# Edge lists in two parts, the mask by four 64x64 products, and the mask one step sooner

## The chip, the cores and the metric

The kernel runs on one NeuronCore of a Trainium2 chip. The metric is the device time of one execution in microseconds (us). Engines are named as in the profile: PE is TensorE's matmul, PEld its weight load, DVE is VectorE, ACT is ScalarE, POOL is GpSimd, SP is SyncE; a "q" behind a name is that engine's sequencer, which issues DMAs.

## The reference

One layer of a graph network over N = 1250 nodes of 512 values, 8 heads of 64, and 41250 edges (`src`, `dst`, sorted by `dst`) with 8 weights each. In short:

```
xn = layernorm(x)
x_norm = layernorm(xn) * g + b;  q, k, v = x_norm @ Wq/Wk/Wv + bias
ws[e, h] = (q[origin] . k[destination])[h] * SCALE * w[e, h]
att = softmax of ws over all edges of one origin
values[origin] += att * v[destination];  gnn = xn + (values @ W1 + b1) @ W2 + b2
mix = linear attention of xn (elu + 1 features), @ Wp + bp
x = x + gnn + mix
out = x + ffn(layernorm(x))      # a small table step on 51 columns
```

## The kernel before

The kernel turns the sparse attention into a dense one. A table `w_tab` in HBM has a row for each of 1280 origins and 1360 columns: 1250 destinations and 110 spare ones ("losers", edges that share a cell with another). Every cell has 8 weights. It is first filled with a marker `EMPTY`, then the weights of the edges are scattered into it.

**The table (SP, DVE, POOL).** SP loads both edge lists into `sW` and `dW` with a halo of 65 (`load_edges`, L410): 22 chunks of 1875 edges on 125 partitions. Chunk 0 needs ten one-row transfers beside. SP then goes through the chunks: it loads the weights of chunk k (`load_weights_of_edges`, L431) and fills a strip of the table with the marker (`empty`, L419). DVE turns the lists into numbers (`edges`, L1187, all 22 chunks in one go) and finds the losers of chunk k (`detect(k)`, L1195: a comparison of 960 values on each partition, a reduction, two small steps), which gives the cells and counts up `s_idx`. POOL scatters 15 rows of cells a chunk (L514), when the chunk's strip, weights and cells are there. After all chunks it gathers the losers' weights (16 transfers, L520), scatters them (16, L525), and then gathers key and value rows of the losers (`KVx`, L587, one of ten for each block of origins, the first three at once).

**The dense start (ACT, PE, DVE).** ACT issues the loads of `x`, then `Wq`, then six short columns (`crow`, L607). PE turns the columns (L903), DVE copies them (L1287), PE folds a bias through `Wq` (`fold(0)`, L873), transposes the normed `x` (L852), and projects q (L884), k, v (L890) in three pieces of 512, 512 and 256 nodes. DVE takes k and v (`take_k` L1276, `take_v` L1281), with a `detect` between each two. `marker_check` (L1208) looks at the edge weights in `V`'s place, so the v tiles wait for it. ACT copies transposed k rows and stores them with v to HBM. All this is in program order on each engine. The linear attention follows, up to 362 us.

**The attention.** 30 rounds w: three groups of destinations (512, 512, and 226 + 110 spare), each over ten blocks c of 128 origins. A round has four steps p = 0 to 3, one for each pair of heads; u = 4w + p. In a step PE does `scores(u)` (two heads, K = 64, side by side in the two row halves of the array, L1085, in the third group also L1088; then the mask, L1090: an identity times `pen`, added to both score banks), `values(u - 2)` (L1118, two heads side by side in the two column halves) and `transposes(u - 1)` (L1100). DVE does `weighted(u)` (scores times weights with the running maximum, twice, L1540, and the shift, L1544), `odd_probs(u - 1)` (a copy that `values` needs, L1549), and at p = 1 of the second and third group `merge(w - 1)` (L1562 to L1574), at p = 2 of the third `scaled`, at p = 3 of the third `added`. ACT does the exponentials (L765) and the other copy (L772). PE does the closing product `ffn` (L1147) at p = 3 of the third group. From round 11 on there is a merge in every round, from round 21 on an `ffn`.

`mask(w + 1)` (L1529) compares one head's weights of the next tile with the marker and writes `pen`, 128 x 512 of bf16, at the end of DVE's step p = 2. It waits for the tile's load. SP loads the tile of w + 1 (`load_tile`, L451) as soon as `weighted` of round w - 1 is through with the same buffer (two buffers `Wt`); the tile is 2048 KB in the first two groups.

Of the kernel before, what the change touches and what calls it, by code (L numbers as in the profile page):

```python
# [8 lines left out]
ALU = mybir.AluOpType  # L9
# [35 lines left out]
GROUPS = ((0, 512), (512, 512), (1024, COLS - 1024))  # L45
READY = (10, 19, 22)
NW = 3 * NT
NU = NW * 4
# [63 lines left out]
def gps_layer(nc, x, src, dst, w_edge, ln_g, ln_b, Wq, bq, Wk, bk, Wv, bv, W1, b1, W2, b2,  # L112
# [3 lines left out]
    with ctx:  # L116
# [127 lines left out]
        KTx = [ar(13312 + 440 * i, 440).rearrange("p (k n) -> p k n", k=KC) for i in range(2)]  # L244
        pen = [ar(14192 + 256 * i, 256).bitcast(BF16) for i in range(2)]
        tb = ar(14704, 512)
        fo = ar(19520, 512)
# [29 lines left out]
        s_pad = sem("pads_ready")  # L277
        s_edges = sem("edges_loaded")
        s_x = [sem(f"x_loaded{j}") for j in range(3)]
# [58 lines left out]
        s_wl = [sem(f"tile_loaded{i}") for i in range(2)]  # L338
        s_pen = sem("mask_ready")
        s_s = sem("scores_ready")  # L340
        s_ttr = sem("weighted_ready")
# [64 lines left out]
        def _(sp):  # L406
# [3 lines left out]
            def load_edges():  # L410
                for a, to in ((src, sW), (dst, dW)):
                    sp.dma_start(to[:, 1:NCH, :], view(a, CE - HALO, ((CJ, QL), (CE, NCH - 1), (1, WIN)))).then_inc(s_edges, 16)
                    sp.dma_start(to[5:QL, 0, :], view(a, 5 * CJ - HALO, ((CJ, QL - 5), (1, WIN)))).then_inc(s_edges, 16)
                sp.wait_ge(s_pad, 1)
                for a, to in ((src, sW), (dst, dW)):
                    for q in range(5):
                        sp.dma_start(to[q:q + 1, 0, HALO - CJ * q:WIN], view(a, 0, ((1, 1), (1, CJ * (q + 1))))).then_inc(s_edges, 16)

            def empty(k):  # L419
# [11 lines left out]
            def load_weights_of_edges(k):  # L431
                if k > 4:
                    scattered(sp, max(k - RING + 1, (k - 3) * 5 // 8))
                sp.dma_start(pay[:, k % RING, :, :], wq[k]).then_inc(s_pay[k % 4], 16)

            sp.dma_start(sWk, wv(Wk)).then_inc(s_w4[1], 16)
            load_edges()
            for k in range(3):
                load_weights_of_edges(k)
                empty(k)  # L440
            sp.wait_ge(s_idx, 1)
            sp.dma_start(wchk, w_edge.rearrange("(p t) h -> p t h", p=QL)).then_inc(s_chk, 16)
# [31 lines left out]
            with sp.If(sp.value_load(flag[0:1, 0:1], min_val=0, max_val=P) > 0):  # L474
                scattered(sp, NCH - 1)
                sp.wait_ge(s_xs, 16 * SLOTS)

            for w in range(NW):
                load_tile(w)
            for b in range(2):  # L480
# [4 lines left out]
        def _(pool):  # L485
# [20 lines left out]

            for k in range(NCH):
                if k >= 2:
                    pool.wait_ge(s_sc[k % 2], 16 * CJ * (k // 2))
                pool.wait_ge(s_empty[k % 4], emptied(k))  # L510
                pool.wait_ge(s_pay[k % 4], 16 * (k // 4 + 1))
                pool.wait_ge(s_idx, k + 1)
                for j in range(CJ):
                    pool.indirect_dma_start(out=w_tab, out_offset=bass.IndirectOffsetOnAxis(ap=idx[:, k, j:j + 1], axis=0),  # L514
                                            in_=pay[:, k % RING, j, :], in_offset=None,
                                            bounds_check=CELLS - 1, oob_is_err=False).then_inc(s_sc[k % 2], 16)

            pool.wait_ge(s_lists, 2)
            for j in range(SLOTS):
                pool.indirect_dma_start(out=wx[:, j, :], out_offset=None, in_=w_edge,  # L520
                                        in_offset=bass.IndirectOffsetOnAxis(ap=e_idx[:, j:j + 1], axis=0),
                                        bounds_check=E - 1, oob_is_err=False).then_inc(s_wx, 16)
            pool.wait_ge(s_wx, 16 * SLOTS)
            for j in range(SLOTS):
# [67 lines left out]
        def _(act):  # L592
# [11 lines left out]
            act.dma_start(XRES[:, 2:4, :], x[2 * P:4 * P, :].rearrange("(t p) d -> p t d", p=P)).then_inc(s_x[0], 16)  # L604
            act.dma_start(sWq, wv(Wq)).then_inc(s_w4[0], 16)
            for i, a in enumerate((ln_g, ln_b, bq, bk, mbq, b1)):
                act.dma_start(crow[KC * i:KC * i + KC, :], a.rearrange("(k p) -> k p", p=P)).then_inc(s_col, 16)  # L607
            load_x(1)

# [218 lines left out]
        def _(pe):  # L828
# [242 lines left out]
            def scores(u):  # L1071
                w, p = u // 4, u % 4
                g, c = w // NT, w % NT
                d0, n = GROUPS[g]
                if p == 0:
                    pe.wait_ge(s_pen, w + 1)
                    if g == 2:
                        pe.wait_ge(s_kxe, c + 1)
                bs = [bank[SB[(2 * u + hh) % 3]] for hh in range(2)]
                if u >= 1:  # L1080
                    pe.wait_ge(s_ttr, 2 * u - 1)
                qs = [QT[64 * hh:64 * hh + 64, p, c * P:(c + 1) * P] for hh in range(2)]
                m = min(n, N - d0)
                for hh in range(2):
                    mm(bs[hh][:, 0:m], qs[hh], KT[64 * hh:64 * hh + 64, p, d0:d0 + m], start=True, stop=False)  # L1085
                if g == 2:
                    for hh in range(2):
                        mm(bs[hh][:, m:n], qs[hh], KTx[c % 2][64 * hh:64 * hh + 64, p, :], start=False, stop=False)  # L1088
                for hh in range(2):
                    last = mm(bs[hh][:, 0:n], identb[:, :], pen[w % 2][:, 0:n], start=False, stop=True)  # L1090
                last.then_inc(s_s, 1)
# [85 lines left out]
        def _(dve):  # L1177
# [8 lines left out]

            def edges():  # L1187
                dve.wait_ge(s_edges, 16 * 14)
                v.tensor_copy(oc[:, :, :], sW[:, :, HALO:WIN])
                ch.link(v.tensor_copy(dc[:, :, :], dW[:, :, HALO:WIN]))  # L1190
                v.scalar_tensor_tensor(out=key, in0=sW, scalar=float(N), in1=dW, op0=ALU.mult, op1=ALU.add)
                v.tensor_copy(dwin, dW)
                ch.link(v.scalar_tensor_tensor(out=cell, in0=oc[:, :, :], scalar=float(COLS), in1=dc[:, :, :], op0=ALU.mult, op1=ALU.add))

# [92 lines left out]
            v.tensor_copy(cols[:, :, :].rearrange("p i k -> p (i k)"), bank[7][:, 32:32 + 6 * KC]).then_inc(s_cols, 1)  # L1287
            normed(0)
            dve.wait_ge(s_cols, 1)
            take_x(0)  # L1290
            fold(0)
            moments(1)
            normed(1)
            edges()
            detect(0)
            detect(1)
            fold(1)
# [226 lines left out]
            def mask(w):  # L1524
                n = GROUPS[w // NT][1]
                dve.wait_ge(s_wl[w % 2], 16 * (w // 2 + 1))
                if w >= 2:
                    dve.wait_ge(s_s, 4 * (w - 1))
                v.tensor_scalar(pen[w % 2][:, 0:n], Wt[w % 2][:, 0:n, 0], EMPTY, -BIG, ALU.is_equal, ALU.mult).then_inc(s_pen, 1)  # L1529

# [115 lines left out]
            for u in range(NU + 8):  # L1646
# [9 lines left out]
                if p == 2 and 2 * NT < w <= NW:  # L1656
                    scaled(w - 1 - 2 * NT)
                if p == 2 and w < NW - 1:
                    mask(w + 1)
# [42 lines left out]
```

## Time and profile before

| | us |
|---|---|
| median of 3 runs (lowest, highest) | 853.5 (851.43, 857.59) |
| the profiled execution's own time | 854.37 |
| its span in the profile | 851.2 |
| PE, DVE, ACT, POOL busy | 782.4, 583.2, 339.6, 457.5 |
| attention begins (first mask on DVE) | 361.96 |

The profile is of one execution, 3.2 us of whose time lie outside the span. Busy times are sums over the span. The chain view goes back from the last instruction to what released each one. In timeline rows the bracket gives the engine's idle time just before and what ended it.

### The profile page before, as it was taken

The numbers are of one execution on the slowest core, as the hardware profiler recorded it, in microseconds if no ns is written. First come the engines' busy times: TensorE is split into PE (matmuls) and PEld (weight loads), VectorE is DVE, ScalarE is ACT, GpSimd is POOL, SyncE is SP. The second block draws the span as 40 slices with busy tenths as digits, with TensorE's granted clock in tenths as the row PEclk, the third lists the DMA queues.
The fourth block names the chain that finished last, engine by engine and source line by source line (L and its number), as shares of the span: only waits on it lengthen the run. The fifth ranks groups of instructions, "written<-read, shape, count | busy, mean of one in ns | idle before, by whom it ended". The sixth has DMA issues, their size and how long they took to land.

```text
span 851.2 us, 13484 instructions
## 1 busy us (share of the span) xinstructions
PE 782.4 (92%) x4751; PEld 458.3 (54%) x4791; DVE 583.2 (69%) x1331; ACT 339.6 (40%) x794; POOL 457.5 (54%) x391
## 2 busy tenths in 40 slices
PE   2999897899999999979999999999999999999993
PEld 2554445444446444435555555555556667666661
DVE  3487594954233503358888888998988978878886
ACT  0311301022312122035556555556555555545662
POOL 1028878778778877777777787777610001001000
PEclk9989999998999999979999999999999999999998
DMA  7697968897546569315353535435354143242203
GB/s 225 175 375 269 320 203 277 250 357 227 161 136 200 158 185 335 95 15 193 103 202 104 185 120 160 146 103 193 108 164 165 66 152 104 95 148 89 86 1 120
DMA packets 69632, 143.98 MB, mean 169 GB/s; under 512 B 20537, under 2 KB 54251, under 8 KB 65599
## 3 DMA queue, kind: packets, MB, share of 16 engines
q1 hardware_dynamic: 47084, 119.42, 39.9%
q0 software_dynamic: 13344, 6.28, 6.6%
q10 hardware_dynamic: 9136, 17.39, 6.2%
q8 instruction: 40, 0.66, 0.3%
q14 instruction: 28, 0.23, 0.1%
HBM read 77.99 MB, written 64.77 MB: 168 GB/s over the span
## 4 chain that ended last, share of the span: by engine, by line
PE 70%; DVE 21%; DMA 4%; issue 3%; ACTq 1%; ACT 1%; DVEq 0%
PE bank L890 17%; PE bank L884 12%; DVE AR L1540 11%; PE bank L1118 8%; PE bank L1085 8%; PE bank L1100 8%; PE bank L1090 4%; PE bank L1147 4%; DVE AR L1549 3%; DMA AR<-w_tab 2%; PE bank L998 2%; PE bank L873 1%; DMA AR<-in_L_gnn_b_dram 1%; PE bank L987 1%; PE bank L949 1%
## 5 line engine op out<-in xcount | busy, mean ns | idle before, releaser
L514 POOL DMA_INDIRECT w_tab<-pay,idx x330 | 403.9, 1224 | 153.3 <-issue 153.0
L765 ACT ACTIVATE AR<-AR,nmx 128x512 f32<-128x512 f32 (+1 forms) x240 | 159.0, 664 | 48.0 <-DVE nmx L1544 46.5
L1540 DVE CUSTOM_DVE_ANT_0 AR<-bank,AR,MX 128x512 f32<-128x512 f32 (+1 forms) x160 | 151.8, 986 | 20.0 <-PE bank L1090 19.1
L772 ACT ACTIVATE AR<-bank 128x512 f32<-128x512 f32 (+1 forms) x120 | 67.3, 561 | 173.9 <-PE bank L1100 173.9
L1085 PE MATMUL bank<-KT,QT 64*128 64x512 f32 (+1 forms) x480 | 118.3, 570 | 8.6 <-issue 5.3
L1100 PE MATMUL bank<-ident,AR 128*128 128x128 f32 (+2 forms) x880 | 122.7, 280 | 1.1 <-ACT AR L765 1.1
L1118 PE MATMUL bank<-AR,V 128*64 128x128 f32 (+1 forms) x1600 | 114.0, 280 | 6.1 <-DVE AR L1549 6.0
L884 PE MATMUL bank<-AR 128*128 128x512 f32 (+1 forms) x288 | 109.0, 538 | 7.3 <-ACT QT L642 3.2
L1118 PEld LDWEIGHTS bank<-AR,V 128*64 128x64 f32 (+1 forms) x1600 | 85.6, 136 | 52.3 <-issue 50.9
L890 PE MATMUL bank<-AR 128*128 128x512 f32 x240 | 108.3, 607 | 2.5 <-ACT AR L696 2.5
L1100 PEld LDWEIGHTS bank<-ident,AR 128*128 128x128 f32 (+2 forms) x880 | 94.0, 139 | 22.3 <-issue 15.9
L1540 DVE CUSTOM_DVE_ANT_0 AR<-bank,AR 128x512 f32<-128x512 f32 x80 | 83.9, 1086 | 29.7 <-PE bank L1090 29.6
L587 POOL DMA_INDIRECT AR<-kv_rows,xd x10 | 10.8, 1075 | 163.2 <-PE bank L1118 157.7
L884 PEld LDWEIGHTS bank<-AR 128*128 128x128 f32 x288 | 55.5, 195 | 56.2 <-issue 48.4
L890 PEld LDWEIGHTS bank<-AR 128*128 128x128 f32 x240 | 46.0, 195 | 57.3 <-issue 54.6
L1549 DVE COPY AR<-bank 128x512 f32<-128x512 f32 (+1 forms) x120 | 76.7, 639 | 0.2 <-PE bank L1100 0.2
L1090 PE MATMUL bank<-AR,identb 128*128 128x512 bf16 (+1 forms) x200 | 58.4, 358 | 6.5 <-DVE AR L1549 4.3
L1085 PEld LDWEIGHTS bank<-KT,QT 64*128 64x128 f32 x480 | 36.6, 186 | 35.9 <-issue 24.1
L1090 PEld LDWEIGHTS bank<-AR,identb 128*128 128x128 bf16 x240 | 13.7, 97 | 66.4 <-issue 62.1
L765 ACT ACTIVATION_READ_ACCUMULATOR AR<-AR,nmx 128x1 f32 x240 | 45.0, 188 | 0.0
L1147 PE MATMUL bank<-AR 128*128 128x512 f32 x80 | 36.1, 594 | 0.8 <-DVE AR L1581 0.8
L890 PE MATMUL bank<-AR,QMN 128*128 128x512 f32 x80 | 35.9, 593 | 0.5 <-DVE QMN L1444 0.5
(250 smaller groups left out, 755.2 us busy)
## 6 DMA issues: line engine op xcount, KB each, us to landing
w_tab<-ztile SPq DMA_DIRECT2D x20, 2280.0 KB, 15.0
AR<-w_tab SPq DMA_DIRECT2D x20, 2048.0 KB
AR<-w_tab SPq DMA_DIRECT2D x10, 1344.0 KB
w_tab<-ztile SPq DMA_DIRECT2D x3, 1800.0 KB, 13.2
w_tab<-pay,idx POOLq DMA_INDIRECT x330, 4.4
w_tab<-ztile SPq DMA_DIRECT2D x2, 1700.0 KB, 16.5
kv_rows<-AR ACTq DMA_DIRECT2D x9, 256.0 KB, 6.5
kv_rows<-V ACTq DMA_DIRECT2D x9, 256.0 KB
```

The costliest lines, as they stand in the source:

```text
L514: pool.indirect_dma_start(out=w_tab, out_offset=bass.IndirectOffsetOnAxis(ap=idx[:, k, j:j + 1], axis=0), in_=pay[:, k % RING, j, :], in_o ...
L765: act.activation(ws[u % 2][hh][:, 0:n], ws[u % 2][hh][:, 0:n], ACT.Exp, bias=nmx[:, u % 4, hh:hh + 1], accum_out=DG[g][:, c, 2 * p + hh:2 ...
L772: act.activation(PT[u % 2][0][:, 0:nb * P], bank[2][:, 0:nb * P], ACT.Copy).then_inc(s_ea, 1)
L884: last = mm(b[:, 0:n], w[:, k, m * P:(m + 1) * P], src_t(k), start=(k == 0), stop=(k == KC - 1))
L890: last = mm(b[:, :], src_t(k), w[:, k, :], start=(k == 0), stop=(k == KC - 1))
L1085: mm(bs[hh][:, 0:m], qs[hh], KT[64 * hh:64 * hh + 64, p, d0:d0 + m], start=True, stop=False)
L1090: last = mm(bs[hh][:, 0:n], identb[:, :], pen[w % 2][:, 0:n], start=False, stop=True)
L1100: last = nc.tensor.transpose(bank[2 + hh][0:rws, i * P:(i + 1) * P], ws[u % 2][hh][:, a:a + rws], ident[:, :])
L1118: last = mm(bank[4 + w % 2][64 * hh:64 * hh + 64, p * P:(p + 1) * P], v, PT[u % 2][hh][0:rws, i * P:(i + 1) * P], start=(i == 0), stop=(i ...
L1147: last = mm(bank[7][:, :], tb[:, k * P:(k + 1) * P], W12[:, k, :], start=(k == 0), stop=(k == KC - 1))
L1540: v.tensor_tensor_reduce(out=ws[u % 2][hh][:, 0:n], in0=bank[SB[(2 * u + hh) % 3]][:, 0:n], in1=Wt[w % 2][:, 0:n, h], scale=1.0, scalar=MX ...
L1549: v.tensor_copy(PT[u % 2][1][:, 0:nb * P], bank[3][:, 0:nb * P]).then_inc(s_ed, 1)
```

## The change

- The edge lists are loaded and turned in two parts: chunks 0 to 3 first, 4 to 21 after. SP's order becomes: first part, weights and fill of chunk 0, `Wk`, second part, then chunks 1 and 2 as before. DVE does the first part and `detect(0)` before `take_x(0)`, `detect(1)` before `moments(1)`, the second part where all of it stood.
- SP waits for `s_idx` 3 in place of 1 before it loads over the edge lists.
- ACT issues the six columns ahead of `Wq`.
- POOL gathers the losers' weights ahead of chunk 20, in place of after chunk 21.
- The mask product: an identity of 64 x 64 in each quarter of the array, four products of 512 columns in place of two of 128 x 128. Two of them need `pen` with its partition halves swapped: two DMAs of 64 partitions a round, issued by SP (`swap_halves`), into `pens`. PE waits for them at p = 0.
- `mask(w + 1)` moves from DVE's step p = 2 to p = 1, and also waits that the swap of two rounds ago is through. SP's order in the attention becomes swap of w, load of tile w + 1.

```diff
+FIRST = 4
...
+        pens = [bias_row[1 + i][:, 0:256].bitcast(BF16) for i in range(2)]
...
             def load_edges():
                 for a, to in ((src, sW), (dst, dW)):
-                    sp.dma_start(to[:, 1:NCH, :], view(a, CE - HALO, ((CJ, QL), (CE, NCH - 1), (1, WIN)))).then_inc(s_edges, 16)
+                    sp.dma_start(to[:, 1:FIRST, :], view(a, CE - HALO, ((CJ, QL), (CE, FIRST - 1), (1, WIN)))).then_inc(s_edges, 16)
...
+            def load_other_edges():
+                for a, to in ((src, sW), (dst, dW)):
+                    sp.dma_start(to[:, FIRST:NCH, :], view(a, FIRST * CE - HALO, ((CJ, QL), (CE, NCH - FIRST), (1, WIN)))).then_inc(s_edgesb, 16)
...
+            load_edges()
+            load_weights_of_edges(0)
+            empty(0)
             sp.dma_start(sWk, wv(Wk)).then_inc(s_w4[1], 16)
-            load_edges()
-            for k in range(3):
+            load_other_edges()
+            for k in range(1, 3):
                 load_weights_of_edges(k)
                 empty(k)
-            sp.wait_ge(s_idx, 1)
+            sp.wait_ge(s_idx, 3)
...
+            def swap_halves(w):
+                n = GROUPS[w // NT][1]
+                sp.wait_ge(s_pen, w + 1)
+                if w >= 2:
+                    sp.wait_ge(s_s, 4 * (w - 1))
+                for i in range(2):
+                    sp.dma_start(pens[w % 2][64 * i:64 * i + 64, 0:n], pen[w % 2][64 - 64 * i:128 - 64 * i, 0:n]).then_inc(s_pens[w % 2], 16)
+
+            load_tile(0)
+            load_tile(1)
             for w in range(NW):
-                load_tile(w)
+                swap_halves(w)
+                if 1 <= w < NW - 1:
+                    load_tile(w + 1)
...
             for k in range(NCH):
+                if k == NCH - 2:
+                    pool.wait_ge(s_lists, 1)
+                    for j in range(SLOTS):
+                        pool.indirect_dma_start(out=wx[:, j, :], out_offset=None, in_=w_edge,
...
-            act.dma_start(sWq, wv(Wq)).then_inc(s_w4[0], 16)
             for i, a in enumerate((ln_g, ln_b, bq, bk, mbq, b1)):
                 act.dma_start(crow[KC * i:KC * i + KC, :], a.rearrange("(k p) -> k p", p=P)).then_inc(s_col, 16)
+            act.dma_start(sWq, wv(Wq)).then_inc(s_w4[0], 16)
...
+                if p == 0:
+                    pe.wait_ge(s_pens[w % 2], 32 * (w // 2 + 1))
                 for hh in range(2):
-                    last = mm(bs[hh][:, 0:n], identb[:, :], pen[w % 2][:, 0:n], start=False, stop=True)
+                    for to in range(2):
+                        a, b = 64 * hh, 64 * to
+                        last = mm(bs[hh][b:b + 64, 0:n], identb[a:a + 64, a:a + 64], (pen if hh == to else pens)[w % 2][a:a + 64, 0:n], start=False, stop=True)
...
             normed(0)
+            edges(0, FIRST)
+            detect(0)
             dve.wait_ge(s_cols, 1)
             take_x(0)
             fold(0)
+            detect(1)
             moments(1)
             normed(1)
-            edges()
-            detect(0)
-            detect(1)
+            edges(FIRST, NCH)
             fold(1)
...
                 if w >= 2:
                     dve.wait_ge(s_s, 4 * (w - 1))
+                    dve.wait_ge(s_pens[w % 2], 32 * (w // 2))
...
-                if p == 2 and w < NW - 1:
+                if p == 1 and w < NW - 1:
                     mask(w + 1)
```

## Rows read from the trace of the kernel before

**Rows 1.** The chain that ended last, 0 to 60 us: start, us, what.
```profile
5.79 9.94 DMA AR<-in_L_gnn_b_dram
...
16.57 6.96 PE bank L873 x32
...
29.47 14.02 PE bank L884 x32
```
**Rows 2.** Timeline of SP's queue, 0 to 60 us: start, us, what it issues.
```profile
1.79 20.65 SPq L413 DMA_DIRECT2D V<-in_src_dram  x1
```
**Rows 3.** DMA queues, 4 to 16 us: packets, MB, share of 16 engines.
```profile
q10 hardware_dynamic: 1565, 3.00, 77.4%
q1 hardware_dynamic: 873, 0.71, 19.3%
```
**Rows 4.** The same view, 18 to 28 us.
```profile
q1 hardware_dynamic: 2996, 0.95, 40.0%
```
**Rows 5.** The same view, 46 to 52 us.
```profile
q1 hardware_dynamic: 1623, 2.19, 104.4%
```
**Rows 6.** Timeline of DVE, up to 82 us.
```profile
42.13 0.33 DVE L1189 CAST oc<-V 125x330 f32<-125x330 int32 x1 [5.47 <-DMA V<-in_dst_dram]
...
47.35 1.15 DVE L1198 TENSOR_REDUCE QMN<-QMN 125x15 f32<-125x960 bf16 x1
...
56.83 0.75 DVE L1276 TENSOR_SCALAR KT<-bank,kbias 128x512 f32<-128x512 f32 x1 [3.02 <-PE bank L884]
...
81.18 0.46 DVE L1210 TENSOR_SCALAR QMN<-V 125x330 f32<-125x330 f32 x1 [4.25 <-DMA V<-in_edge_attr_dram]
```
**Rows 7.** The chain in the first group, 425 to 442 us: one step of PE.
```profile
432.60 1.06 PE bank L1085 x4
433.66 0.54 PE bank L1090 x2
434.20 1.02 PE bank L1118 x16
435.22 1.02 PE bank L1100 x8
```
**Rows 8.** Timeline of SP's queue in the first group: the issue of one tile.
```profile
425.54 0.32 SPq L463 DMA_DIRECT2D AR<-w_tab  x1
```
**Rows 9.** Windows: length, each engine's busy us (instructions), PE clock, DMA share, GB/s.
```profile
427.50:433.40 5.90, 5.74 (x49) 3.47 (x46) 5.10 (x12) 2.94 (x9) 4.68 (x5) 1.00 0.84 317
433.40:434.00 0.60, 0.60 (x4) 0.11 (x2) 0.21 (x1) 0.60 (x3) 0.30 (x2) 1.00 0.00 0
```
**Rows 10.** Timeline of DVE in the first group.
```profile
432.93 0.68 DVE L1549 COPY AR<-bank 128x512 f32<-128x512 f32 x1
434.34 1.09 DVE L1540 CUSTOM_DVE_ANT_0 AR<-bank,AR 128x512 f32<-128x512 f32 x1 [0.73 <-PE bank L1090]
...
437.16 0.61 DVE L1529 TENSOR_SCALAR AR<-AR 128x512 bf16<-128x512 f32 x1
```
**Rows 11.** The chain in the second group, 556 to 573 us.
```profile
563.70 1.15 DVE AR L1540
...
571.69 1.09 PE bank L1118 x16
```
**Rows 12.** Timeline of DVE in the second group: the mask.
```profile
571.46 0.62 DVE L1529 TENSOR_SCALAR AR<-AR 128x512 bf16<-128x512 f32 x1
```
**Rows 13.** The chain in the third group, 694 to 711 us.
```profile
702.13 0.83 DVE AR L1540
...
708.81 0.88 PE bank L1118 x12
```
**Rows 14.** The chain over the whole span: a tile's load in the second group.
```profile
620.69 13.98 DMA AR<-w_tab
```
**Rows 15.** Timeline of POOL: its first scatter, and the first gather of losers' rows.
```profile
57.47 1.39 POOL L514 DMA_INDIRECT w_tab<-pay,idx  x1 [53.06 <-issue]
...
617.51 1.14 POOL L587 DMA_INDIRECT AR<-kv_rows,xd  x1 [4.92 <-issue]
```
**Rows 16.** POOL's scatters by source line: from issue to landing.
```profile
DMA to landing us min/median/max: 2.4/4.4/9.2
```

More of the change, by code:

```diff
@@ L277, in gps_layer @@
         s_pad = sem("pads_ready")
-        s_edges = sem("edges_loaded")
+        s_edges = sem("first_edges_loaded")
+        s_edgesb = sem("other_edges_loaded")
         s_x = [sem(f"x_loaded{j}") for j in range(3)]
@@ L339, in gps_layer @@
         s_pen = sem("mask_ready")
+        s_pens = [sem(f"mask_halves_swapped{i}") for i in range(2)]
         s_s = sem("scores_ready")
@@ L507, in _ @@
             for k in range(NCH):
+                if k == NCH - 2:
+                    pool.wait_ge(s_lists, 1)
+                    for j in range(SLOTS):
+                        pool.indirect_dma_start(out=wx[:, j, :], out_offset=None, in_=w_edge,
+                                                in_offset=bass.IndirectOffsetOnAxis(ap=e_idx[:, j:j + 1], axis=0),
+                                                bounds_check=E - 1, oob_is_err=False).then_inc(s_wx, 16)
                 if k >= 2:
@@ L516, in _ @@
                                             bounds_check=CELLS - 1, oob_is_err=False).then_inc(s_sc[k % 2], 16)
+            pool.wait_ge(s_wx, 16 * SLOTS)
             pool.wait_ge(s_lists, 2)
[L519 to L523, printed above, removed]
             for j in range(SLOTS):
@@ L1185, in _, with edges @@
             v.memset(wx[:, :, :], 0.0)
[L1187 to L1193, printed above, removed]
+            def edges(a, b):
+                if a == 0:
+                    dve.wait_ge(s_edges, 16 * 14)
+                else:
+                    dve.wait_ge(s_edgesb, 32)
+                v.tensor_copy(oc[:, a:b, :], sW[:, a:b, HALO:WIN])
+                ch.link(v.tensor_copy(dc[:, a:b, :], dW[:, a:b, HALO:WIN]))
+                v.scalar_tensor_tensor(out=key[:, a:b, :], in0=sW[:, a:b, :], scalar=float(N), in1=dW[:, a:b, :], op0=ALU.mult, op1=ALU.add)
+                v.tensor_copy(dwin[:, a:b, :], dW[:, a:b, :])
+                ch.link(v.scalar_tensor_tensor(out=cell[:, a:b, :], in0=oc[:, a:b, :], scalar=float(COLS), in1=dc[:, a:b, :], op0=ALU.mult, op1=ALU.add))
             def detect(k):
```

## The prediction

> **What bounds the kernel now.** I read the chain of waits first, over the whole span and then in short windows. At the start it hangs on the last short column, which lands 9.9 us after its issue; then `fold(0)` at 16.57 and the q projection at 29.47 [rows 1]. From there to the attention PE hardly pauses, so what PE starts sooner stays sooner. In the first group of the attention the chain is PE alone: a step is 1.06 + 0.54 + 1.02 + 1.02 = 3.64 us, a round 14.6 [rows 7], and DVE idles 0.73 in a step [rows 10]. In the second group the chain changes engines: from DVE's `weighted` of p = 1 (563.70) DVE alone leads to PE's `values` at 571.69, 7.99 us [rows 11]; the other 7.5 of a round's 15.5 are PE, two steps. In the third group the DVE part is 702.13 to 708.81, 6.68 [rows 13], of a round of 16.3. These DVE parts hold the merge, which stands at p = 1. POOL bounds nothing: its gather at 617.51 [rows 15] is well ahead of the third group.
>
> **The start.** Columns ahead of `Wq`, and `Wk` (1 MB) no longer ahead of everything. Between 4 and 16 us the DMA engines were full (77.4 + 19.3%) and q10, ACT's queue with x and `Wq`, moved 3.00 MB [rows 3], 250 GB/s. Without `Wk` beside it `x` should land 1.5 to 2 us sooner, the columns before 11, and `Wq` (1 MB, 4 us at that rate) at 12 to 13. `fold(0)` then starts when DVE has copied the columns and `Wq` is there, at about 13.5 in place of 16.57: 3 us gained. Bounds: 5 us gained (it follows the columns alone), 1 lost (the fill of chunk 0, 3.4 MB, halves `Wq`'s rate). I take 3, nearest to [rows 3].
>
> On DVE `edges(0, 4)` (4/22 of the work, about 1 us) and `detect(0)` (two steps of 1.15 and two small ones, 2.7 [rows 6]) come ahead of `take_x(0)`. DVE has them between about 16 and 20, and `take_x(0)` is due at 23: hidden, if the first lists are there by 19. They are 1000 packets; SP's queue managed 873 in 12 us beside ACT's [rows 3] and 300 per us alone [rows 4], so 10 to 16. `detect(1)` (2.7) ahead of `moments(1)` is hidden behind 14 us of q projection [rows 1].
>
> The second part of the lists is what moves later. Before, the issue of the lists held SP for 20 us [rows 2] and DVE had them at 42.13 after 5.47 of waiting [rows 6]. Now 3.4 MB of fill stand in front, 9.3 us at 2.19 MB in 6 us [rows 5]: I expect them at 52 (50 to 57). Behind DVE's wait stand `fold(1)`, the order checks and `take_k(0, 0)`; with 3.4 + 2.2 us of work that comes at 58, where PE, 3 us sooner, has the product ready at 54. PE does not wait for it, since v's first product needs that bank some 13 us later. By the time DVE reaches the v tiles it waited 4.25 us for the weights to check [rows 6], and this room takes up the rest. SP's later count (3 of `s_idx`) comes at about 62, when its queue is still full of fills. Cost 0; each us past 57 costs one.
>
> **POOL.** Its first scatter moves from 57.47 to about 25, but chunk 1 needs the fill behind the second part, at about 62 where chunk 1 began at 80. It ends some 18 to 20 us sooner; nothing waits for that. The gather of loser weights only changes its place. What it does move is the gather of losers' rows: at 617.51 [rows 15] it stretched one tile load to 13.98 us [rows 14] from some 8, for which the mask at p = 2 waited 1.3. It will come near 597, again beside a tile load more likely than not (8 of 15 us are loads), and the mask at p = 1 is due 9 to 10 us after a load's issue in this group. I add 1.5 (between -1.3, no collision, and 4).
>
> **The mask product.** Four products of 512 columns, 64 x 64, in place of two. The trace shows no 64 x 64. Nearest rows: two row halves run side by side (four 512-column passes in 1.06, 0.27 each [rows 7], where the full array takes 14.02/32 = 0.44 [rows 1]), and two column halves as well (16 passes of 128 columns in 1.02, as many us as 8 transposes [rows 7]). One product with its switch is 0.54/2 = 0.27. Bounds: 0.27 (all at once) and 1.08 (one after another). I take 0.36, one product and 0.03 for each that starts behind it, since both halvings are seen to overlap: 0.18 gained a step, in the third group 0.13.
>
> A rule of the Trainium skill speaks against it ("TensorE: Matmul & The Clock Gate", Part 3: Packing small matmuls): a weight load overlaps running matmuls only where the row group differs. By it the two quarters of one row half would take turns and the product would gain nothing. Rows 7 disagree for column halves, which share all rows and still take half the time; by the rule the sum is rival B's.
>
> **The swap.** Two DMAs of 64 KB a round. The mask will be done some 6 us before `scores` of the next p = 0 ask for it; the scatters, small as well, land in 2.4 to 9.2 us, median 4.4 [rows 16]. Cost 0, up to 0.3 a round in a bad case. PE's wait has only PE's own queue behind it.
>
> **The mask one step sooner.** First group (rounds 0 to 10, no merge): the load is issued at 425.54 [rows 8], the DMA engines run until about 433.4 and then stand still [rows 9], so it lands about 8.0 after its issue. DVE would reach the mask after the copy of p = 1 at 432.93 + 0.60 = 433.53 [rows 10], 8.0 after the issue, and, with steps 0.18 shorter, at 7.7. So it waits 0.3, then 0.55, against a slack of 0.73 - 0.18: `weighted` of p = 2 comes about 0.4 late, PE can take 0.2 of it. A round gains 4 x 0.18 - 0.2 = 0.5, eleven rounds 5.7.
>
> Second group (rounds 11 to 20, nine such): the mask now stands behind the merge, inside the DVE part of the chain, in front of `weighted` of p = 2 and the copy that `values` waits for. Before it stood behind that copy (571.46 against PE's 571.69 [rows 11, 12]). The DVE part grows by 0.54, the PE part shrinks by 2 x 0.18: +0.18 a round, +1.6. The load is there (it has 9 us). Third group, nine rounds: the mask of 336 columns adds 0.38, two PE steps give back 0.26: +0.12, +1.1.
>
> **Sum:** -3 - 5.7 + 1.6 + 1.1 + 1.5 = -4.5. The profiled execution becomes 854.4 - 4.5 = 849.9; it was 0.9 above the median of the runs, so 849.0.
>
> **Rivals.**
> A, the forecast, 849.0, 66%; its own range 843 to 855.
> B, the four products overlap only in pairs: the group stays at 0.54. No gain in the first group, +0.54 x 9 and +0.38 x 9 in the others, with -3 and +1.5: +6.8, 860.3, slower. Place: L1090. For it: two quarters share one row half's stream, and no row shows both halvings at once. Against it: rows 7. Some 74 steps count (44 + 18 + 12), so the change loses as soon as the group takes over 0.36 + 4.5/74 = 0.42. One after another (1.08) would be 38 us more than now. 13%.
> C, the second part of the lists comes at 64, since its 320-byte packets starve beside ACT's loads (873 packets in 12 us [rows 3] against 2996 in 10 [rows 4]): `take_k` and `take_v` hold PE, 7 us: 856. Against it: between 18 and 28 us ACT's queue is empty, and 3000 of the 4500 packets fit into such a stretch. 13%.
> D, the mask's new place costs nothing and PE bounds every step: 80 x 0.18 + 40 x 0.13 = 19.6, with -3 and +1.5: 833. Against it: rows 11 and 13, where no PE work stands in the DVE part. 8%.
> That the change does what it says in POOL's order is sure and worth nothing here.
>
> **How the numbers follow.** A measurement of this kernel tells about 1% (8.5 us) from no change: 845 and 862 are the marks. Faster by more: D, and a good fifth of A where the start gives 5 and the group takes 0.30: 0.28. Slower: the worse half of B, a little of C and of A: 0.12. The rest 0.60. The range 840 to 861 leaves out D and the worse half of B.
>
> **What would show it.** The q projection starts at 26 to 27; the first `detect` stands before it; DVE's second part starts at 50 to 57 and PE has no new gap before 130. A step of the first group takes 3.45 to 3.5 us, L1090's share 0.36. DVE has a short wait of the mask on the tile load in rounds 1 to 10 (0.3). Second-group rounds are 15.6 to 15.7, third-group 16.4, with the mask right behind L1574. POOL's first loser-row gather is near 597. Wrong: L1090 above 0.42 a step, a PE gap near 60 to 85 us behind `take_k` or `take_v`, or rounds of the second group under 15.3.

## The result, and the profile after

| | us |
|---|---|
| kernel before, median of its runs beside this comparison | 853.1 |
| changed kernel, median of 4 runs (857.66 to 861.48) | 860.14 |
| ratio, with its 95% interval | 1.0076 [1.0053, 1.0099] |
| forecast | 849.0, range 840 to 861 |
| profiled execution after: own time, span | 857.66, 855.9 (before 854.4, 851.2) |

Here and below, executions over 1.5% slower than the fastest of their kernel are left out (two of r3, one of r14).

The change makes the kernel 7 us slower, where I expected it to be 4 us faster; the profiled execution after is itself 2.5 us below its median. Now from the start of the span to its end, by when `weighted` (L1574, once L1540) begins each part. The first round of the attention begins 3.3 us later than before (371.83 against 368.57), round 10 only 0.3 later (514.81 against 514.52), round 20 later by 4.0 (673.55 against 669.53), and the end by 4.7. So the attention's first group wins 3.0 (forecast 5.7), but the start and the second group lose.

**The start works, and its lead is gone 150 us later.** The chain that ended last, 0 to 55 us (start, us, what; here and below the pieces called issue of under 0.1 us are left out):

```profile
5.30 8.37 DMA AR<-in_L_gnn_Wq_dram
13.72 6.99 PE bank L898 x32
...
42.67 0.50 ACT AR L658
43.21 1.14 PE bank L877 x8
44.35 6.23 PE bank L898 x32
50.58 11.76 PE bank L909 x22
```

`fold(0)` starts at 13.72 in place of 16.57 [rows 1], and now waits for `Wq`. The q projection follows at 26.45, 3.0 sooner than [rows 1] have it. At 43.21 the chain passes through ACT (L658): `detect(1)` stands in front of `moments(1)`, so ACT is late with the tiles that the second x transposes need, and PE waits 1.45 us. That little pause comes with more, as the windows of the stretch show (us, busy time of each engine with its instructions, PE clock, DMA share, GB/s), of the changed kernel:

```profile
43.00:55.00 12.00, 11.79 (x46) 9.14 (x47) 0.00 (x0) 1.73 (x4) 5.74 (x5) 0.57 0.50 118
```

PE is granted 0.57 of its clock here, with 1.2 GHz (a granted 0.5) lasting 10.2 us from 44.7; in the kernel before it lasted 6.8 us from 48.6. `fold(1)` takes 6.39 us where it took 4.67, and k's projection begins at 50.44 against 50.87 (both by the timeline of PE): of 3.0 us, 0.4 are left. Some of it comes back in small waits (2.1 ahead at 161.5). DVE's second part of the lists is where I had it, with no wait of PE behind it. The timeline of DVE:

```profile
56.40 0.30 DVE L1221 CAST oc<-V 125x270 f32<-125x270 int32 x1 [19.56 <-DMA V<-in_dst_dram]
```

The large loss is at 162. The chain, 160 to 190 us, in the changed kernel:

```profile
162.28 14.21 DMA AR<-in_L_mix_Wk_dram
176.49 4.07 issue
180.56 0.56 PE bank L952 x2
```

This is the `Wk` of the linear attention (`L_mix_Wk`, 1 MB; the expectations below also call it the second layer's). It takes 14.2 us to land. Before, the same load took 7.8 (165.1 to 172.9), and no one waited for it. It is not the last that PE waits for: in the kernel PE waits for `Wk` and `Wv` together, ahead of L952, and the 4.07 of issue are the rest of `Wv`'s load. ACT issues `Wv` right behind `Wk`:

```profile
163.17 2.20 ACTq L707 DMA_DIRECT2D AR<-in_L_mix_Wv_dram  x1
```
```profile
AR<-in_L_mix_Wv_dram ACTq DMA_DIRECT2D x1, 1024.0 KB, 17.3
```

163.17 + 17.3 is 180.47, and PE starts at 180.56; before, `Wv` took 10.5 and was there at 176.1, 3 us before PE came to it. Where `Wk` is named below, `Wv` lands 3 to 6 us after it, and where PE waits it is `Wv` that ends the wait. SP's queue shows what is different:

```profile
161.69 0.52 SPq L437 DMA_DIRECT2D w_tab<-ztile  x1
162.31 1.11 SPq L442 DMA_DIRECT2D pay<-in_edge_attr_dram  x1
163.47 2.21 SPq L437 DMA_DIRECT2D w_tab<-ztile  x1
```

Two fills of 2.3 MB stand right beside it. In the kernel before, SP issued a fill at 154.68 and the next at 178.24, so that `Wk` and `Wv` went through between them. The fills wait for POOL's scatters of an earlier chunk, POOL's chunk 1 now starts at 64 in place of 81, and with that the whole sequence of fills lies elsewhere against ACT's loads. The timeline of PE has the price, and the windows the clock behind it:

```profile
180.56 0.56 PE L952 MATMUL bank<-QMN,tri 125*125 125x10 f32 x2 [5.07 <-issue]
```
```profile
177.80:184.60 6.80, 4.04 (x8) 2.36 (x9) 2.63 (x11) 4.66 (x7) 5.41 (x5) 0.50 1.05 390
```

PE idles 5.07 us and then runs 6.8 us at half clock, while the DMA engines are full (share 1.05). A lead of 2.1 has become a lag of 3.3.

**The mask's product.** The chain in the first group, 443 to 447 us, against [rows 7]:

```profile
443.65 1.06 PE bank L1110 x4
444.71 0.34 PE bank L1119 x4
445.05 1.02 PE bank L1147 x16
446.08 1.02 PE bank L1129 x8
```

0.34 us for four products, where two of the full array took 0.54; 0.36 was my term. All four run at once, by the timeline of PE (start, duration):

```profile
444.64 0.40 PE L1119 MATMUL bank<-AR,identb 64*64 64x512 bf16 x1
444.64 0.40 PE L1119 MATMUL bank<-bias_row,identb 64*64 64x512 bf16 x2
444.65 0.40 PE L1119 MATMUL bank<-AR,identb 64*64 64x512 bf16 x1
```

They start within 0.01 us. The Trainium skill ("TensorE: Matmul & The Clock Gate", Part 3: Packing small matmuls) says that a weight load overlaps running matmuls only where the row group differs. By that rule, as the prediction had weighed it, the two quarters of one row half would take turns; here they don't, and by the trace the four weight loads (0.10 to 0.11 us each) start in the same 0.01 us as well.

**The mask's wait for its tile** was on my list with 0.3, and is larger. Timeline of DVE, one round of the first group:

```profile
437.66 0.93 DVE L1563 TENSOR_SCALAR AR<-AR 128x512 bf16<-128x512 f32 x1 [0.93 <-DMA AR<-w_tab]
```

and the chain over the first group, with the tile loads that have come onto it:

```profile
385.49 8.89 DMA AR<-w_tab
...
428.61 9.03 DMA AR<-w_tab
457.69 8.21 DMA AR<-w_tab
```

I had counted 8.0 us from issue to landing, from one round [rows 8, 9]. The first four that are on the chain (two of them stand here) take 8.8 to 9.0, and their masks wait 0.73 to 1.25; later loads take some 8 and most masks wait under 0.6. An undisturbed round is 13.79; the first ten average 14.30, against 14.60 before.

**Second and third group** came as worked out. Second: 15.62 a round (15.49 before), with the mask in DVE's part of the chain, where it was not in [rows 11]:

```profile
568.25 0.70 DVE QMN L1608
568.98 0.04 DVE AR L1563
569.01 0.51 issue
569.53 1.12 DVE AR L1574
```

(The mask's own record lasts 0.63 us; the chain books 0.04 of it to the mask and the rest to issue.)

Third: 16.42 (16.30 before). The collision of the losers' gather with a tile load, by the chain:

```profile
605.93 11.86 DMA AR<-w_tab
617.87 0.06 DVE AR L1563
```

The gather was at 602.31 (617.51 in [rows 15], 597 forecast). The load took 11.86, the mask waited 2.06 and PE 2.79; then the granted clock was 0.51 for 3.5 us, as the windows show:

```profile
621.50:625.00 3.50, 3.47 (x24) 3.16 (x24) 2.18 (x5) 0.85 (x4) 0.00 (x0) 0.51 0.29 61
```

This round has 19.21 in place of 15.62, so 3.6, against 1.1 that the collision of [rows 14] had cost in two rounds (16.37 and 15.73 in place of 15.49). The two DMAs of a swap, last, are cheap (DMA issues of the page: KB each, median us to landing):

```profile
bias_row<-AR SPq DMA_DIRECT2D x40, 64.0 KB, 2.0
```

### The profile page after: what moved, and what is told of

The parts are those of the page before. It is cut to its first block, busy times and chain, and to the rows that moved or that the text cites. A ratio compares the mean times of both kernels' runs of the same rounds, so it can differ in the third digit from the quotient of the medians.

```text
span 855.9 us, 14118 instructions
## 1 busy us (share of the span) xinstructions
PE 774.2 (90%) x5031; PEld 462.0 (54%) x5031; DVE 584.9 (68%) x1336; ACT 338.7 (40%) x794; POOL 460.6 (54%) x391
## 4 chain that ended last, share of the span: by engine, by line
PE 58%; DVE 22%; DMA 12%; issue 4%; ACT 2%; ACTq 1%; DVEq 0%
PE bank L915 17%; DVE AR L1574 12%; DMA AR<-w_tab 8%; PE bank L909 8%; PE bank L1147 6%; PE bank L1129 6%; PE bank L1110 6%; PE bank L1176 4%; DVE AR L1583 3%; PE bank L1119 2%; DMA AR<-in_L_mix_Wk_dram 2%; PE bank L1023 2%; PE bank L898 2%; PE bank L1012 1%; DMA AR<-in_L_gnn_Wq_dram 1%
## 5 line engine op out<-in xcount | busy, mean ns | idle before, releaser
L1574 DVE CUSTOM_DVE_ANT_0 AR<-bank,AR,MX 128x512 f32<-128x512 f32 (+1 forms) x160 | 151.4, 983 | 16.9 <-PE bank L1119 16.9
L797 ACT ACTIVATE AR<-bank 128x512 f32<-128x512 f32 (+1 forms) x120 | 67.3, 561 | 162.1 <-PE bank L1129 161.5
L909 PE MATMUL bank<-AR 128*128 128x512 f32 (+1 forms) x288 | 107.2, 531 | 5.8 <-ACT QT L667 2.3
L1574 DVE CUSTOM_DVE_ANT_0 AR<-bank,AR 128x512 f32<-128x512 f32 x80 | 83.9, 1085 | 21.9 <-PE bank L1119 21.7
L1119 PEld LDWEIGHTS bank<-AR,identb 64*64 64x64 bf16 x240 | 13.6, 103 | 67.0 <-issue 62.8
L1119 PE MATMUL bank<-AR,identb 64*64 64x512 bf16 (+1 forms) x240 | 46.8, 380 | 0.0
L1119 PE MATMUL bank<-bias_row,identb 64*64 64x512 bf16 (+1 forms) x240 | 46.0, 380 | 0.0
```

Of the source, the lines that this page charges most:

```text
L797: act.activation(PT[u % 2][0][:, 0:nb * P], bank[2][:, 0:nb * P], ACT.Copy).then_inc(s_ea, 1)
L909: last = mm(b[:, 0:n], w[:, k, m * P:(m + 1) * P], src_t(k), start=(k == 0), stop=(k == KC - 1))
L1119: last = mm(bs[hh][b:b + 64, 0:n], identb[a:a + 64, a:a + 64], (pen if hh == to else pens)[w % 2][a:a + 64, 0:n], start=False, stop=True)
L1574: v.tensor_tensor_reduce(out=ws[u % 2][hh][:, 0:n], in0=bank[SB[(2 * u + hh) % 3]][:, 0:n], in1=Wt[w % 2][:, 0:n, h], scale=1.0, scalar=MX ...
```

## The experiments

Theory S: POOL's earlier phase puts the fills beside the linear attention's `Wk` and `Wv` and eats more than the lead. Rival M: the mask part is what makes it slower. Later rivals stand with the runs. Each comparison gives its ratio to the kernel before, run on the same chip beside it: 852.9 for the first four runs, 860.4 for the second four, 852.6 and 854.7 for the third and fourth. The times of r1, r4, r13 and r14 came out 0.9 to 2.6 us outside what their theory had said; the waits that it named came or went as it said. Larger misses stand with their runs.

**The two halves of the change, apart.** `r1_start_only`: start and POOL's order as changed, the mask by two full products at p = 2 and without the swap:

```diff
                 for hh in range(2):
-                    for to in range(2):
-                        a, b = 64 * hh, 64 * to
-                        last = mm(bs[hh][b:b + 64, 0:n], identb[a:a + 64, a:a + 64], (pen if hh == to else pens)[w % 2][a:a + 64, 0:n], start=False, stop=True)
+                    last = mm(bs[hh][:, 0:n], identb[:, :], pen[w % 2][:, 0:n], start=False, stop=True)
...
-                if p == 1 and w < NW - 1:
+                if p == 2 and w < NW - 1:
```

> The start part and the new order on POOL alone, the mask as before. Theory S (the start loses what it gains, because the fills run ahead of their old phase and the loads of the linear attention's weights land late): the attention begins 3 to 4 us later than before though the q projection begins 3 us sooner; time 856 to 858 against 853.5. Rival M (the start is worth its 3 us and the whole loss lies in the mask part): 850 to 851.

Measured: 859.7, 1.0067 [1.0010, 1.0123]. `Wk` took 15.15 us, PE idled 8.5 us, the attention began at 377.4, 8.8 later than before; its rounds were those of before (14.58, 15.48, 16.30). I ran it a second time, `r12_start_again`:

> The new start with the mask as before, products two at a time. On a chip where the kernel before takes 853 it takes 857 to 861 once more. On one where that takes 860, theory Q (the four products at a time are what that chip slows) says 864 to 868, and the rival (the start, or the chip alone whatever the mask) 890 or more.

859.7 again, 1.0077 [1.0052, 1.0103]; the chain and the timeline of PE in that run:

```profile
166.70 15.62 DMA AR<-in_L_mix_Wk_dram
```
```profile
187.64 0.56 PE L948 MATMUL bank<-QMN,tri 125*125 125x10 f32 x2 [7.23 <-issue]
```

So the start alone, meant to win 3 us, costs 7. `r2_mask_only` is the other half: the old start (with `Wq` and the gather of the losers' weights in their old places as well) and the new mask.

```diff
-            load_edges()
-            load_weights_of_edges(0)
-            empty(0)
...
-            load_other_edges()
-            for k in range(1, 3):
+            load_edges()
+            for k in range(3):
...
-            edges(0, FIRST)
-            detect(0)
...
-            edges(FIRST, NCH)
+            edges(0, NCH)
+            detect(0)
+            detect(1)
```

> The mask part alone (four 64x64 products, swap, mask at p = 1), the start and POOL as before. Theory S: first group -3, second and third +1.3 and +1.1, the late load beside the losers' gather +2 to +3: 855 to 857. Rival M: 860 or more.

Measured: 855.23, 1.0033 [1.0002, 1.0063]; rounds 14.61 on average, 15.64 and 16.43, the mask waiting up to 1.8 for its tile. Rival M, as the source of the 7 us, is out: the mask part costs 2 to 3, at the edge of its interval.

**What in the start costs it.** `r4_pool_held` gives POOL its old phase back:

```diff
                 if k == 1:
+                    pool.wait_ge(s_pr, PROJ_OF["v", 2] + 1)
```

> After, but POOL's chunk 1 waits until PE has made v of tile 2 (some 80 us, where it began before). Theory S: the fills fall back to their old phase, the load of the linear attention's Wk takes 8 us again in place of 14, PE's gap of 5.1 us at 180 is gone, the attention begins 4 us sooner than in after: 855 to 857. Rival (the late load has another cause, such as the order of the first fills): the gap stays, 860.

Measured: 857.86, 1.0050 [1.0028, 1.0072]. `Wk` lands after 7.2 us, and the wait at 180 is gone. SP's queue has the gap between the fills back:

```profile
151.63 0.52 SPq L437 DMA_DIRECT2D w_tab<-ztile  x1
176.18 0.26 SPq L442 DMA_DIRECT2D pay<-in_edge_attr_dram  x1
176.48 0.52 SPq L437 DMA_DIRECT2D w_tab<-ztile  x1
```

The attention begins at 367.97, 3.9 sooner than in the changed kernel. The time is only 2 to 3 us below the changed kernel's, since the gather, at 614.3, now made one round 20.16.

`r13_fills_again` takes the collision away by the fills themselves and leaves POOL early. This edit and the next ran first on another chip (below).

```diff
                 load_weights_of_edges(k)
+                if k == 11:
+                    sp.wait_ge(s_mv_l, 16)
                 empty(k)
```

> The changed kernel, with the fill of chunk 11 (and all behind it on SP's queue) held until the second layer's Wv has landed. Theory S (fills ahead of the Wk load cost the lead): Wk lands within 9 us of its issue, the PE gap at 177 to 190 us (5 to 8 us in the changed kernel) is gone, the attention starts at 364 to 368 in place of 371 to 375, and the time is 853 to 857. Rival D (ScalarE's late x transposes at 43 us are the loss): the time stays at 858 to 862. Should the chip be the one on which all of these took 37 us more, only the first 365 us count.

Measured: 850.38, 0.9947 [0.9920, 0.9974]: one wait on one fill takes the ratio from 1.0076 to 0.9947, some 11 us, and makes of the change a gain of half a per cent. SP's queue, and PE at the place of the wait:

```profile
172.31 0.52 SPq L437 DMA_DIRECT2D w_tab<-ztile  x1
```
```profile
174.71 0.28 PE L954 MATMUL bank<-QMN,tri 125*125 125x10 f32 x2
```

`Wk` landed 7.8 us after its issue, `Wv` 10.2, and the attention began at 362.6, 6.0 sooner than before. Of these, 2.7 stood at PE's q projection of the linear attention (160.90 against 163.58), and 1.7 more came in it: it took 13.97 us at a granted 1.00 behind a wait of 1.83, where the kernel before had waited 2.64 us ahead of it, was granted 0.71 up to 166 and 0.50 (1.2 GHz) up to 168, and took 15.67. The last 1.6 I did not trace. `r14_detect_again` puts `detect(1)` behind `normed(1)` again. It tests the expectations' rival D (ACT's late transposes; not the D of the prediction):

```diff
             fold(0)
-            detect(1)
             moments(1)
             normed(1)
+            detect(1)
```

> The changed kernel with detect(1) behind normed(1) again. The wait of 1.45 us at 43 us goes (both theories). Theory S: the Wk load still meets a fill in most runs, so 856 to 861 with a wide spread, as this moves the queues' phase only by chance. Rival D: 855 or less in every run, with the attention at 366 or sooner.

Measured: 862.6, 1.0075 [1.0048, 1.0102]. The wait of 1.45 at 43 us is 0.44 again, as before the change, and nothing is won. The chain, and PE:

```profile
165.88 15.77 DMA AR<-in_L_mix_Wk_dram
```
```profile
187.03 0.57 PE L952 MATMUL bank<-QMN,tri 125*125 125x10 f32 x2 [9.04 <-issue]
```

This rival D is out. Both edits together, `r15_both_again`:

> Both of these edits, mask where the change has it (p = 1). Theory S: the lead of 3 us lasts to the attention (364 to 366 in place of 368.6 before), then -3 in the first group, +1.3 in the second, +1.1 in the third and +2.5 where a gather meets a load: 849 to 854, what the sum of the prediction would have been with its start kept and the first group's waits at their measured size. Rival (something else in the start or the attention is lost): 857 or more.

Measured: 851.93, 0.9973 [0.9945, 1.0001], as r13 within their spread.

**The mask's place.** `r3_mask_p2`: the changed kernel with the mask back at p = 2.

```diff
-                if p == 1 and w < NW - 1:
+                if p == 2 and w < NW - 1:
```

Theory P says that only the four products pay and the place costs.

> After with mask(w + 1) back at p = 2. Theory P (the place behind the merge and ahead of the tile load costs 0.5 us a round, the swap has room enough): rounds of 13.8, 15.1 and 16.0 us in the three groups, 843 to 846. Rival Q (at p = 2 the swap lands too late for the next p = 0, which is why the mask was moved): PE waits 0.3 to 0.7 at each p = 0, rounds of 14.3, 15.5 and 16.2, 852 to 857.

Measured: 853.0, 1.0014 [0.9979, 1.0048], 7 us above what theory P had said. Undisturbed rounds are 13.79, 15.14 and 16.06, and no mask waits; with p = 1 they are 13.79, 15.62 and 16.42. The first ten average 14.01, where they were 14.30 with p = 1 and 14.60 before. So theory P is right on the rounds, but the swap is not always in time, and its rival Q had a part of it. PE waits for the swap in three of the first ten rounds, here in the worst of them, and in no round of the changed kernel:

```profile
502.41 0.40 PE L1119 MATMUL bank<-AR,identb 64*64 64x512 bf16 x1 [1.02 <-DMA bias_row<-AR]
```

Beside the losers' gather it waits 2.87, and that round takes 18.03, the next 16.68. The start lost the rest again (`Wk` 13.6 us, attention at 376.7). So the old start with this mask looked like the best version: `r10_p2_again`, which is the edit of r3 on the kernel of r2:

> The old start, the new mask one step sooner still (at p = 2 of the round before). Theory C: on a chip where the kernel before takes 853, first group 13.8 a round (from 14.6: -8), second 15.1 (from 15.5: -3), third 16.05 (from 16.3: -2), gather beside a load +2: 842, range 838 to 848. Rival K: 890 or more wherever it runs.

Measured: 852.75, 0.9992 [0.9972, 1.0011]: 10 us above its sum, and not the rival's 890. Rounds 1 to 5 are 13.79, but round 9 has 17.33. The chain there:

```profile
496.49 2.58 DMA w_tab<-pay,idx
499.09 8.96 DMA AR<-w_tab
```

Tile 10's load, which with such rounds was due near 492.5, waits for the scatters of the chunks that the second group reads; then the mask waits 3.33. The two rounds beside the losers' gather are 19.65 and 16.50, 5.9 us more than two of 15.13, and `Wk` took 11.0 us and `Wv` 12.5 behind a fill, for which PE waited 2.06. With the old start and rounds this short POOL is a bound. In the kernel before, whose rounds are longer, that scatter (issued at 492.6, some 4 us sooner than in r10) was in time for a load at 498.5. In the changed kernel it goes out at 479.2, and no load waits.

**The best of both.** `r11_combo_again` is the changed kernel with the fills held, the old place of `detect(1)`, the mask at p = 2, and the first gather of losers' rows behind tile 17's load. Beside the edits of r3, r13 and r14 that is

```diff
+            pool.wait_ge(s_wl[1], 144)
             for c in range(NT):
                 if c >= 3:
```

> The new start with ScalarE's two moments(1)/detect(1) in the old order and the fills held until the second layer's Wv has landed, the mask at p = 2. Theory C: as r10 with the attention 2 to 3 us sooner: 840, range 835 to 848, on a chip where the kernel before takes 853. Rival K: 890 or more.

Measured: 844.59, 0.9901 [0.9871, 0.9931], the best of all, and 1% under the kernel before, where r13 had 0.5%. Without that line, `r16_combo_no_gather`:

> The combination of r11 (old order of detect(1), fills held, mask at p = 2) without the gather's wait for tile 17's load. In r11 the gather was issued at 607.1 and the swap of that round still took 6.1 us, so the wait moved it little: within 2 us of r11's 844.6, so 842 to 848. Rival (the gather's wait carried the gain): 850 or more.

Measured: 848.35, and 0.9904 [0.9868, 0.9940] to the kernel before beside it: the same ratio. The edits of r16 are those of r15 and the mask at p = 2, and r15 ran on the same chip: 851.9 and 0.9973 there, 848.4 and 0.9904 here, so the mask's place alone is worth 4 to 6 us. The gather's wait does nothing: in r11 the gather still went out at 607.1, its round took 19.33 and the next 17.27. That collision is what both still pay. The chain of r16:

```profile
611.26 7.05 DMA bias_row<-AR
618.36 0.64 PE bank L1121 x4
619.00 1.90 PE bank L1149 x16
```

A swap of 64 KB takes 7.05 us beside the gather, in the changed kernel 2.0 (median); PE waits 4.85 for it and goes on at half clock (0.50 for 3.6 us). In six other rounds of r16 up to 541 us PE waits 0.2 to 1.1 for a swap of 2.3 to 3.5 us. Two rounds, 20.24 and 16.87, hold 6.8 us more than two of 15.13.

**One chip of its own.** The control `r9_after_again` is the changed kernel once more:

> The changed kernel as it is, as the control for the four kernels on the other chip, which all took about 37 us more than their sums. Theory C (that chip): the time follows the chip; where the kernel before takes 853, this one takes 858 to 862, and where the kernel before takes 860 it takes 895 to 900, since there TensorE's products are signalled up to 3.1 us later than the trace has them end. Rival K (my variants): what they share, and this kernel has not, costs the 37 us; then it takes 858 to 868 on either chip.

Measured: 861.68, 1.0102 [1.0082, 1.0122], the attention at 375.5. The four kernels below, all run on one other chip, had come out far from their sums. `r5_p2_old_start` is the kernel of r10:

> The four products and the swap with mask(w + 1) at p = 2, and the start and POOL as before. Theory P + S: rounds of 13.8, 15.15 and 16.06 us as in r3, the attention begins as before (368.6), so 853 - 13 = 840. Rival (other rounds than r3's, since POOL's scatters and the losers' gather fall elsewhere, give part of it back): 845 to 850.

`r6_fills_wait` and `r7_detect_back` are those of r13 and r15:

> After, but SP holds the fill of chunk 11 until the linear attention's Wk and Wv have landed; nothing else is touched, POOL stays early. Theory S: that load takes about 8 us in place of 14, the gap at 180 is gone, the attention begins at 367 to 368, 856 to 857. Rival (the late load comes from POOL's scatters or from the v and k rows, not from the fills): the gap stays at 3 us or more, 860.

> r6 with detect(1) behind moments(1) and normed(1) again. Theory D (detect(1) ahead of the moments delays the second transposes, and that is where the start's first lead goes): no gap of 1.4 us at 43, k projection starts 1.5 to 3 us sooner than in r6, and 1.5 to 2.5 us remain at the end: 854 to 855. Rival (the lead is lost to ACT and the clock anyway): as r6 within 0.5 us.

`r8_combo` is that of r11:

> r7 with the mask at p = 2 and the losers' first gathers held until tile 17 has landed. Theory: start 1 to 3 us ahead of before, rounds as in r3 (-13), no late tile load beside the gather (-1 against before): 837 to 840, faster than both kernels. Rival (what r3 showed in two of its ten rounds comes from elsewhere): single rounds of 16 to 18 us stay, 842 to 846.

Measured there: 897.53, 896.78, 898.55 and 893.98, ratios 1.0406 [1.0356, 1.0456], 1.0399, 1.0433 and 1.0380 [1.0334, 1.0426], where the kernel before took 860.4. Elsewhere the same four kernels take 852.8, 850.4, 851.9 and 844.6. Their first 365 us show nothing (the attention begins at 364.7 to 368.0); of the rounds up to about 600 us most take 17 to 20 us, and from then on they are as elsewhere. Windows of PE say that it did less in the same time, with full clock granted; r5 first, the same 60 us of r3 behind it:

```profile
440.00:500.00 60.00, 47.08 (x428) 28.77 (x426) 41.39 (x83) 27.61 (x68) 47.92 (x40) 1.00 0.46 146
```
```profile
440.00:500.00 60.00, 59.51 (x555) 36.84 (x552) 52.42 (x110) 37.28 (x90) 48.06 (x40) 1.00 0.49 154
```

and the timeline of r5 shows where it stands:

```profile
443.79 1.09 PE L1124 MATMUL bank<-ident,AR 128*128 128x128 f32 x8
...
447.77 0.60 ACT L792 ACTIVATE AR<-bank 128x512 f32<-128x512 f32 x1 [3.85 <-remote]
447.77 0.69 DVE L1577 COPY AR<-bank 128x512 f32<-128x512 f32 x1 [1.97 <-remote]
```

The transposes end at 444.9 by the trace, and both copies start at 447.77, 2.9 us after them; in r3, by the same reading, the first copy starts 0.04 us after their end. Matmul ends are modelled, so PE may have been slower than its rows say. What the four share is the product of four at a time and its swap, and no kernel without it but the kernel before was run there, so its share isn't shown and the cause stays open.

## Why the prediction was wrong

- **The start, -3.** The q projection at 26 to 27: right (26.45). The second part of the lists at 50 to 57 without a wait of PE: right (56.4). The step that failed is the sentence that what PE starts sooner stays sooner, and beside it that of the earlier scatters I said nothing waits for them. I followed POOL's and SP's new phase to the gather only. It reaches the fills too, and two fills beside `Wk` and `Wv` make them 6 to 10 us late: `Wk` took 13.6 to 15.8 and `Wv` 17.3 to 19.6 in six executions (the changed kernel twice, r1, r3, r12, r14), 7.2 to 7.8 and 9.7 to 10.5 in r4, r13 and before. Term: +3.3 in the profiled execution, up to +10 in others, in place of -3. With the fills out of the way the attention starts 6.0 sooner in r13 and 3.6, 4.6 and 2.1 in r15, r11 and r16, so the 3 had been there to keep.
- **`detect(1)` ahead of `moments(1)`, 0.** It cost 1.45 us of PE's wait at 43, which was not hidden. By r14 and r15 it doesn't show in the time.
- **The product, 0.36.** Measured 0.34. Rival B, 13%, fell.
- **First group, -5.7.** The mechanism is right, the load's wait was mis-sized: one round's 8.0 us was taken for all, and rounds whose load took 8.8 to 9.0 waited up to 1.25. Measured -3.0; a round in which no load is late is 13.79, 0.79 less than before, but the average is only 0.30 less, where my sum had 0.5.
- **Second and third group, +1.6 and +1.1.** Measured +0.13 and +0.12 a round: right.
- **The gather, +1.5.** Measured +3.6 in its round against the 1.1 of before, so +2.5: the clock behind the wait wasn't in my sum. It came at 602.3, since POOL was 13 to 15 us sooner and not 18 to 20.
- **Rivals C and D of the prediction.** C's 7 us at `take_k` didn't come (lists at 56.4). D needed the mask's place to be free; r3 and r16 show that it isn't. By its own terms D's time is 832, not 833.
- **POOL bounds nothing.** This holds for the kernel before, with 3 us to spare at tile 10's load. r10 shows that with rounds of 13.8 POOL decides when the second group may load.
- **The sum's total** would have stood, its terms not. r13 has what it left out put right: 0.9947, or 4.5 us under its neighbour of 854.7; the forecast had said 4.5. That is luck: by the profiles the start gave 6.0 in place of 3, the first group 2.0 in place of 5.7.

## What to carry to other kernels

A transfer chain that one engine paces (here SP's fills behind POOL's scatters) has a phase. Whoever starts it sooner should list the loads of the other queues that pass between its transfers, over the whole span, and see which of them it will now meet. A gain that is far from its first consumer is worth only what the next tight load leaves of it; one wait on one fill brought it back here. And a place for an operation is chosen by what the chain does there: right behind the merge the mask was on it, one step later it was off it, but its swap then had less room, and PE waited for some of them.

## What the runs showed of the hardware

- Four bf16 products of 64 x 64 in the four quarters of TensorE run together: 0.34 us in the chain for 512 columns each, started within 0.01 us.
- A 1 MB load took 7.2 to 7.8 us where the last fill of 2.3 MB had gone out 10.4 us ahead of it or more (before, r4, r13), 9.2 at 9.4 us (r2), 11.0 at 7.7 us (r10), and 13.6 to 15.8 where two fills went out near it: 0.6 us ahead and 1.2 behind in the changed kernel, both within 5.2 us ahead in r12.
- A DMA of 64 KB from one tile to another lands in 2.0 us (median of 40 in the changed kernel), but took up to 3.5 in the first groups of r11 and r16 and 7.05 beside an indirect gather and a tile's load in r16.
- On one chip the four kernels with such products took 894 to 899 us in place of 845 to 853, and the kernel before 860 in place of 853 to 855. The same comparison can so come out with another sign on one chip of several.
